# Gate batches of a language-model tower overlap, and the top-k constants of its mixer load and are set at other places

## The reference, cut to what matters

```python
# layer 0, first half (x is the layer norm of the embedded tokens h)
u = silu(x @ u_w.T + u_b); v = silu(x @ v_w.T + v_b)
out = irfft(rfft(v) * rfft(kernel))                    # [b, n, 192]
out = u * out @ o_w.T + o_b                            # gate: elementwise product, then projection
x_r = silu(srms((x - out) @ t_w.T + t_b, 192))         # root-mean-square norm over 64 channels
h = h + (x + x_r)
# layer 0, second half (x is the layer norm of h), per head and token
q = x @ Wq_pk; sim = q . pk_keys                       # two halves of 64 keys
scores, idx = top_k(sim, 16); best 16 of the pairs; softmax; gather keys and values
h = h + causal_attention(...) @ Wo
# layer 1: attention and 8 experts, top 2
```

## Time and profile before

| | us |
|---|---|
| median of 3 runs | 3780.31 (3778.2 to 3783.99) |
| the profiled execution | 3773.41 |
| its span, first to last instruction | 3771.6 |
| mean granted TensorE clock | 0.888 of full speed |
| PE busy | 3106.3 (82%) |
| DVE busy | 2982.6 (79%) |
| ACT busy | 2002.6 (53%) |
| POOL busy | 2063.7 (55%) |
| gate stage | 325 to 447 |
| mixer stage | 447 to the end |

### The profile page before, as it was taken

How to read it: one execution, slowest core, us unless ns; L and a number is a source line. 1 busy time by engine, 2 the same in 40 slices (tenths; PEclk the granted TensorE clock), 3 DMA queues, 4 the chain that set the end, 5 groups by cost and what they waited for, 6 DMA issues and landing times.

```text
span 3771.6 us, 42602 instructions
## 1 busy us (share of the span) xinstructions
PE 3106.3 (82%) x10352; PEld 1432.1 (38%) x10352; DVE 2982.6 (79%) x11187; ACT 2002.6 (53%) x4529; POOL 2063.7 (55%) x2084
## 2 busy tenths in 40 slices
PE   3796326689888897989898979898988889899888
PEld 1453102234334343434343434343443343444334
DVE  4443499899999999899898999898979999965322
ACT  2212215566666666656667666566665666566122
POOL 3000017777777777767565777675646776766000
PEclk9997558799899998999998989899988999999666
DMA  0120101222222221212121222121212221211000
GB/s 15 34 67 18 48 12 51 74 56 67 60 61 67 56 69 51 69 44 71 40 69 36 63 57 65 47 65 47 62 38 57 64 63 50 64 51 45 3 0 3
DMA packets 87060, 186.55 MB, mean 49 GB/s; under 512 B 40216, under 2 KB 42173, under 8 KB 86816
## 3 DMA queue, kind: packets, MB, share of 16 engines
q0 software_dynamic: 66560, 135.40, 13.7%
q1 hardware_dynamic: 20256, 48.48, 4.1%
HBM read 182.69 MB, written 1.05 MB: 49 GB/s over the span
## 4 chain that ended last, share of the span: by engine, by line
DVE 44%; PE 33%; issue 5%; ACT 3%; POOL 2%; DMA 1%; SPq 0%; DVEq 0%; ACTq 0%; POOLq 0%
DVE mx_W L1382 9%; PE mx_acc L1052 8%; PE mx_O L1064 6%; DVE mx_G L1539 5%; PE mx_area L1098 4%; DVE mx_mx_part L1562 3%; POOL mx_G L1021 2%; DVE mx_S L1399 2%; PE mx_D L1042 2%; DVE mx_I L1398 2%; DVE mx_hot L1509 1%; PE mx_area L1114 1%; DVE mx_row L1511 1%; DVE mx_V L1394 1%; PE mx_area L1128 1%
## 5 line engine op out<-in xcount | busy, mean ns | idle before, releaser
L1021 POOL DMA_INDIRECT mx_G<-in_kv_table,mx_slot_i x2048 | 2032.7, 993 | 1396.3 <-issue 553.5
L1052 PE MATMUL mx_acc<-mx_W,mx_table 128*128 128x512 f32 x2048 | 1129.0, 634 | 0.0
L1299 ACT ACTIVATE mx_G<-mx_G,mx_slot_w 128x128 f32<-128x128 f32 x2048 | 702.8, 395 | 313.8 <-DMA mx_G<-in_kv_table,mx_slot_i 313.8
L1382 DVE SCALAR_TENSOR_TENSOR mx_W<-mx_D,mx_W 128x512 f32<-128x512 f32 x1024 | 704.1, 688 | 159.8 <-ACT mx_W L1233 126.5
L1233 ACT ACTIVATE mx_W<-mx_D 128x512 f32<-128x512 f32 x1024 | 605.7, 592 | 350.0 <-PE mx_D L1042 344.1
L1042 PE MATMUL mx_D<-mx_U,mx_pick_b 96*128 96x512 bf16 x1024 | 415.5, 406 | 191.1 <-DVE mx_W L1382 190.5
L1052 PEld LDWEIGHTS mx_acc<-mx_W,mx_table 128*128 128x128 f32 x2048 | 418.6, 206 | 199.3 <-issue 103.5
L1257 ACT ACTIVATE mx_PT<-mx_area 128x512 f32<-128x512 f32 x480 | 243.7, 508 | 324.8 <-PE mx_area L1102 176.2
L1064 PE MATMUL mx_O<-mx_PT,mx_KVs 128*65 128x512 f32 (+3 forms) x768 | 313.9, 490 | 9.2 <-ACT mx_PT L1257 7.4
L1539 DVE TENSOR_TENSOR mx_G<-mx_G 128x1024 f32<-128x1024 f32 (+2 forms) x384 | 299.6, 780 | 17.5 <-ACT mx_G L1299 5.6
L1078 PE MATMUL mx_area<-mx_KTa,mx_QTa 64*128 64x512 f32 (+3 forms) x384 | 202.7, 612 | 124.0 <-DVE mx_mx_part L1562 81.7
(11 more groups left out here) (343 smaller groups left out, 4667.5 us busy)
## 6 DMA issues: line engine op xcount, KB each, us to landing
mx_table<-in_kv_dense SPq DMA_DIRECT2D x64, 512.0 KB, 3.6
mx_G<-in_kv_table,mx_slot_i POOLq DMA_INDIRECT x2048
cv_table<-in_c_idft SPq DMA_DIRECT2D x12, 512.0 KB, 3.3
cv_table<-in_c_dft SPq DMA_DIRECT2D x6, 512.0 KB, 3.4
cv_table<-in_c_idft SPq DMA_DIRECT2D x4, 256.0 KB, 3.2
out_h<-mx_xc SPq DMA_DIRECT2D x4, 256.0 KB
mx_G<-in_c_pick SPq DMA_DIRECT2D x1, 672.0 KB
st_h<-in_tok_W,em_ids POOLq DMA_INDIRECT x32, 2.4
```

Of the source, the lines that this page charges most:

```text
L1021: pool.indirect_dma_start(G[g % RING][:, r, :], None, a["kv_table"], bass.IndirectOffsetOnAxis(slot_i[n % 2][:, k, r:r + 1], 0))\
L1052: pe.matmul(acc[:, :], table[:, tile, :], W[c % TILE_RING][:, :], start=(tile == 0), stop=(tile == TILES - 1)).then_inc(applied, 1)
L1299: last = act.activation(rows, rows, ACT.Copy, scale=slot_w[n % 2][:, k, i:i + 1])
L1382: dve.scalar_tensor_tensor(W[c % TILE_RING][:, :], D_ps[c % 3][:, :], 0.0, W[c % TILE_RING][:, :], ALU.is_ge, ALU.mult).then_inc(w_done, 1)
```

## The change

The gate stage loses its hardware loops and is written out for the 4 batches, with other orders on each engine. PE does `gated(b + 1)`, which is steps 2 and 4 of the next batch, between step 6 of this batch and step 8 of this batch. ACT does step 3 of the next batch right behind the Silu of this one. DVE does step 5 of the next batch and step 1 of the batch after that behind its layer norm. The transposes of `xn` go to `uyT2_ps` and no longer to `outT_ps`. A copy of `xn` back to the tile of the same name in the outer scope (L696) is gone. SP issues the loads of `pk_w` and `keys` in the gate stage, into tiles that live as long as the program. In the mixer PE, ACT and DVE no longer wait at the start: they do so at position 18, where DVE also sets the constants.

```diff
@@ gate_stage, SP
+            sp.dma_start(st["pk_w"][:, :, :], a["pk_w"].rearrange("p (c k) -> p c k", c=HP)).then_inc(keys_in, 16)
+            sp.dma_start(st["keys"][:, :, :], a["pk_keys"].rearrange("p (c k) -> p c k", c=HP)).then_inc(keys_in, 16)
+            sp.wait_ge(keys_in, 32)
@@ gate_stage, PE
-            with pe.Fori(0, B) as b:
+            def gated(b):
                 pe.wait_ge(uy_ready, b + 1)
+                if b >= 2:
+                    pe.wait_ge(xnT_copied, b - 1)
                 for t in range(NB):
                     pe.transpose(uyT1_ps[:, t * P:(t + 1) * P], uy[:, t, 0:P], ident[:, :])
                     last = pe.transpose(uyT2_ps[:, t * P:(t + 1) * P], uy[:, t, P:D1], ident[:, :])
                 last.then_inc(uyT_ready, 1)
                 pe.wait_ge(uyT_copied, b + 1)
-                pe.wait_ge(xnT_copied, b + 1)
...
+            gated(0)
+            for b in range(B):
                 pe.wait_ge(dT_ready, b + 1)
...
                 last.then_inc(z_ready, 1)
+                if b + 1 < B:
+                    gated(b + 1)
                 pe.wait_ge(xn_ready, b + 1)
-                flip_rows(pe, outT_ps, xn, ident).then_inc(xnT_ready, 1)
+                flip_rows(pe, uyT2_ps, xn, ident).then_inc(xnT_ready, 1)
@@ gate_stage, ACT
+            def copy_gated(b):
+                act.wait_ge(uyT_ready, b + 1)
+                if b:
+                    act.wait_ge(outT_ready, b)
...
+            copy_gated(0)
+            for b in range(B):
                 act.wait_ge(square_ready, b + 1)
...
                 act.activation(xr[:, :, :], zn[:, :, :], ACT.Silu).then_inc(xr_ready, 1)
+                if b + 1 < B:
+                    copy_gated(b + 1)
                 act.wait_ge(ln_var, b + 1)
@@ gate_stage, DVE
+            gate_rows(0)
+            differ(0)
+            gate_rows(1)
+            for b in range(B):
...
-                chain.link(dve.tensor_copy(st["xn"][:, blocks, :], xn[:, :, :]))
...
+                if b + 1 < B:
+                    differ(b + 1)
+                if b + 2 < B:
+                    gate_rows(b + 2)
@@ mixer_stage, SP
-        N_LOADS = 16
+        N_LOADS = 14
+        CONSTS = 18
...
-                (pk_w[:, :, :], a["pk_w"].rearrange("p (c k) -> p c k", c=HP)),
-                (keys[:, :, :], a["pk_keys"].rearrange("p (c k) -> p c k", c=HP)),
@@ mixer_stage, PE
-            pe.wait_ge(loaded, 16 * N_LOADS)
-            pe.wait_ge(consts_set, 1)
...
             for q in range(SLOTS * SLOT):
                 c = q - SLOT
+                if q == CONSTS:
+                    pe.wait_ge(loaded, 16 * N_LOADS)
+                    pe.wait_ge(consts_set, 1)
@@ mixer_stage, ACT
-            act.wait_ge(consts_set, 1)
             for q in range(SLOTS * SLOT):
                 t, p = divmod(q, SLOT)
+                if q == CONSTS:
+                    act.wait_ge(consts_set, 1)
@@ mixer_stage, DVE: the wait, the casts and memsets are now constants()
                 if p == 0:
                     chain.clear()
+                if q == CONSTS:
+                    constants()
```

More of the change, by code:

```diff
@@ L656, in _ @@
                 act.activation(xr[:, :, :], zn[:, :, :], ACT.Silu).then_inc(xr_ready, 1)
+                if b + 1 < B:
+                    copy_gated(b + 1)
                 act.wait_ge(ln_var, b + 1)
                 act.activation(stat[:, 3, :], stat[:, 0, :], ACT.Sqrt).then_inc(ln_std, 1)
-                act.wait_ge(xnT_ready, b + 2)
-                act.activation(st["xnT"][:, bass.ds(b * N, N)], outT_ps[:, :], ACT.Copy).then_inc(xnT_copied, 1)
-                chain.clear()
+                act.wait_ge(xnT_ready, b + 1)
+                act.activation(st["xnT"][:, b * N:(b + 1) * N], uyT2_ps[:, :], ACT.Copy).then_inc(xnT_copied, 1)
         @block.vector
@@ L665, in _, with gate_rows, differ @@
             chain = Chain(dve, dve_steps)
+            def gate_rows(b):
+                if b:
+                    dve.wait_ge(uyT_ready, b)
+                dve.tensor_tensor(uy[:, :, :], st["u"][:, b * NB:(b + 1) * NB, :], st["y"][:, :, b * D1:(b + 1) * D1],
+                                  ALU.mult).then_inc(uy_ready, 1)
+            def differ(b):
+                dve.wait_ge(outT_ready, b + 1)
+                if b:
+                    dve.wait_ge(z_ready, b)
+                dve.tensor_tensor(dT[0:D, :], st["xnT"][:, b * N:(b + 1) * N], outT_ps[:, :], ALU.subtract)\
+                   .then_inc(dT_ready, 1)
             dve.memset(uyT2[D:D + 1, :], 1.0).then_inc(ones_set, 1)
             dve.memset(dT[D:D + 1, :], 1.0).then_inc(ones_set, 1)
[L668 to L671, removed]
-                   .then_inc(uy_ready, 1)
-                dve.wait_ge(outT_ready, b + 1)
-                dve.tensor_tensor(dT[0:D, :], st["xnT"][:, bass.ds(b * N, N)], outT_ps[:, :], ALU.subtract)\
-                   .then_inc(dT_ready, 1)
+            gate_rows(0)
+            differ(0)
+            gate_rows(1)
+            for b in range(B):
+                blocks = slice(b * NB, (b + 1) * NB)
                 dve.wait_ge(z_ready, b + 1)
@@ L687, in _ @@
                 chain.link(dve.tensor_tensor(xc[:, :, :], h1[:, :, :], xr[:, :, :], ALU.add))
-                chain.link(dve.tensor_copy(st["h"][:, blocks, :], xc[:, :, :]))
+                chain.mark(dve.tensor_copy(st["h"][:, blocks, :], xc[:, :, :]))
                 layernorm_a(dve, chain, xc[:, :, :], h1[:, :, :], sq[:, :, :], stat)
@@ L809, in mixer_stage @@
         pick_b = m.sb("pick_b", [96, 14, P], BF16)
-        pk_w = m.sb("pk_w", [D, HP, P])
-        keys = m.sb("keys", [P, HP, 4 * NK])
+        pk_w, keys = st["pk_w"], st["keys"]
         rank = m.sb("rank", [P, CAND])
@@ L1671, in tower @@
             "xnT": m.sb("xnT", [D, T]),
+            "pk_w": m.sb("pk_w", [D, HP, P]),
+            "keys": m.sb("keys", [P, HP, 4 * NK]),
         }
```

48 lines of the change are left out of this document (23 added, 25 removed).

## The result

The changed kernel takes 3728.92 us in the median of 4 runs (3714.7 to 3733.95), the kernel before, run beside it, 3782.15 (3778.2 to 3785.09, 4 runs). The ratio is 0.9854, with a 95% interval from 0.9823 to 0.9884. The forecast was 3728.6. The difference of the medians is 53.2 us, by the interval 44 to 67.

A forecast was written before the change was run, and what follows sets the result against it. The prediction took the gate stage and the mixer's head as chains on the path, the rest as full. Savings of 38.8 + 12.9 = 51.7 us from 3780.3 gave 3728.6 us, range 3718 to 3743.

The forecast's parts named there:

- the forecast's own case: Gate stage saves 38.8 us and mixer's head 12.9, giving 3728.6 us; chance 0.61.
- The period: Gate stage: time between `z` copies of successive batches, summed to 16.6 us from 29.5, saving 38.8 us over three.
- The mis-sized term: Gate stage: PE's flips of `xn` take 1.7 us per period and hide DVE's 1.21 us for `dT`.
- the point on TensorE's queue: Gate stage: matmuls stay in program order, so `z` can't pass the flips; passing would save 1.5 us in all.
- The sign that the prediction gave beside it: Gate stage: PE goes from projection to flips to `z` without a stop, at a granted clock near 1.
- rival 2: Gate stage: clock stays high, DVE sets a 14.4 us period, 58.3 us saved in all, time 3722.0; chance 0.12.
- The mixer's head: From SP's first mixer issue to k = 15: 35.4 us instead of 48.3, saving 12.9 us.
- the loops: Gate stage: replacing three hardware loops counted at nothing, with up to 0.8 us per DVE turn off the path.
- carried over: Whole kernel: the median lies 6.9 us above the profiled execution before, and the forecast assumed the same after.
- Rival 3: Mixer's head: late loads or the constants leave none of the 12.9 us, time 3741.5; chance 0.06.
- rival 4: Mixer: waits for gathers or table parts lose half the lead, time 3754; chance 0.03.
- rival 5: Mixer: TensorE's clock is granted less and loses 59.3 us or more, so the kernel is slower; chance 0.01.

The follow-up runs named there:

- z_first: The changed kernel with PE doing `z` of the next batch ahead of the flips of this batch: 3725.77 us, ratio 0.9867.
- warm_fill: The changed kernel plus unread matmuls on PE between transposes and projection of batches 1 to 3: 3724.38 us, ratio 0.9843.
- consts_first: The changed kernel with the wait and constants back at position 0, `pk_w` and `keys` still loaded early: 4225.17 us, ratio 0.9893, in the slow session.
- memsets_early: The changed kernel with the constants' memsets moved to positions 0 and 4, only the four casts left at position 18: 3724.03 us, ratio 0.9849.
- written_out: The kernel before with its three gate-stage hardware loops written out, old order, nothing overlapped: 3775.34 us, run once.
- after_same: The changed kernel again, unedited, timed beside `both_again`: 3724.84 us, ratio 0.9856.
- gate_only: The new gate stage with the old mixer head, against the kernel before: 4236.63 us, ratio 0.9912, in the slow session.
- head_only: The old looped gate stage with early loads and the constants at position 18, against the kernel before: 4252.02 us, ratio 0.996, in the slow session.
- both_extra: The changed kernel with the edits of both `warm_fill` and `memsets_early`: 3720.25 us, ratio 0.9834.
- both_again: The kernel of `both_extra` run again, beside `after_same`: 3719.64 us, ratio 0.9837.
- late_start: The kernel of `both_extra` with 14 more scratch memsets on DVE ahead of the gate stage: 3723.34 us, ratio 0.9852.
- the first four experiments: `gate_only`, `head_only`, `consts_first` and `after_again`, measured in one session in which every kernel took 4190 to 4290 us, the one before 4271.75.
- after_again: The changed kernel without an edit, run in the slow session: 4215.9 us, ratio 0.9876.

## Why the prediction was right

The forecast of 3728.6 us was right, within 0.4 us of the median, and the forecast's own case was the one that happened. That it agrees to 0.4 us is luck, as the last point shows; what the prediction can claim is the mechanism and the 51.7 us, for 53.2 measured. By its steps:

- **The period.** From the start of the first `z` copy to that of the second the trace has 4.53 us to the end of the Silu, 1.91 to the projection, 6.89 to DVE's `dT`, 1.21 of `dT` and 2.09 of `z`: 16.63. The forecast had 4.5 + 2.0 + 6.3 + 1.7 + 2.1 = 16.6. The other two periods are 15.13 and 16.12, since the projection takes 5.4 and 6.4 us in them. The stage saved 40.8 us in this execution and 38.8 was forecast; over the profiled executions of the changed kernel it was 47.9 to 49.5 us long, which is 39.1 to 40.8 saved.
- **The mis-sized term** is "1.7" for the flips, with "DVE's 1.21 us for `dT` run beside the flips and are hidden by them". It is the other way round. With the high clock the flips took 1.26 us (356.13 to 357.39) and ended before `dT` (357.54); `z` waited 0.20 us for `dT`. The term on the path is `dT`'s 1.21 us, 0.5 less per period, which is 1.5 of the 1.9 us by which the three periods beat the forecast. The 1.7 came from a spacing of 0.13 us between transposes, read at the rows where the clock was just changing (390.68 to 390.81); at the high level they are 0.11 us apart (359.55 and 359.66 in the trace after), and the flips go from 2.3 to 1.26 us, not to 1.7. From this follows that the point on TensorE's queue was without effect: `z`'s input came last, so no run here shows whether a matmul could pass another, and `z_first` shows PE waiting for `dT` with the flips out of the way.
- **The clock.** The forecast put the projection in the middle between both levels, at 6.3 us, which held for the mean of three (6.9, 5.4 and 6.4): 0.53 to 0.66 in it, 1.00 behind it. The sign that the prediction gave beside it, a clock near 1 from the projection on, contradicts its own 6.3 and didn't come. The "pause of some 3 us per period" was 3.3 us once and 4.7 twice. `warm_fill` shows that this pause is what brings the clock down: with matmuls in it the projection is at 1.00 and the mechanism of rival 2 takes over, with a period of 13.6 where 14.4 was worked out. Of the 0.8 us between them 0.5 is again the 1.7, since `z` started 1.2 us behind `xn`, and 0.2 is the way up to `xn`, 10.4 us for 10.6. The Trainium skill, "TensorE: Matmul & The Clock Gate", part 1, which calls throttled the default state that activity releases, agrees with this run.
- **The mixer's head** saved 12.9 us as forecast (48.34 to 35.40), and every run with this head took 35.39 to 35.41. The constants were an unbroken block of 8.5 us on DVE, 26.8 us behind SP's first issue, with no wait for a transfer. `consts_first` shows the place of the constants, which hides the wait for the other loads, as the larger part, and `memsets_early` that 7.1 of the 8.5 us could go as well.
- **Costed at nothing**: the loops. The forecast allowed "up to 0.8 us of gain per turn of DVE's loop (...), off the path now". `written_out` shows 1.6 us per turn in the old order, 0.6 of it that idle time. This isn't an error of the sum, because the new period was rebuilt from durations that held no loop, but it bears on what the 38.8 us are owed to: if the loops would cost the same in the new order, which no run shows, some 4.9 us of the stage's 39.1 to 40.8 come from them and some 35 from the order. The copy at L696, put at nothing, was never tried alone.
- **The rest**. The mixer from k = 15 to the end was to keep its length, 3276 us. In the profiled execution it took 3272.6, in `after_same` 3280.5. The step "carried over" added 6.9 us from the profiled execution to the median; after the change the median lies 14.2 above the profiled execution, 7.3 more. The profiled execution itself (3714.7) was 7.0 under the forecast for it, 3721.7. These two misses cancel in the forecast of the median. Of the 7.0, 2.0 are the stage, 3.7 the mixer, 1.0 that its first `z` copy came earlier (343.00 for 344.00) and 0.3 the way from the last one to SP's issue.

Of the other signs, the wait at `uyT2_ps` did not come (ACT's copy to `xnT` ends at 358.46, the next transposes start at 359.43), k = 0 came 5.5 us behind SP's issue for 5.7, and two of the three periods were within the 16 to 17 us.

Rival 3 (nothing of the head), rival 4 (half of the lead lost) and rival 5 (slower) did not occur; `gate_only` and `head_only` together show both parts in the result.

## What to carry to other kernels

A stage in which no engine is busy half of the time is a chain: write down one period from the rows, each piece with the wait that ends it, and let the next batch's work start in the waits; the sum then gave the time to 1.5 us per batch here. In such a stage TensorE's clock is a term of its own, since a pause of 3.3 to 4.7 us ahead of a matmul group here doubled the time of its first matmuls, and of two chains of nearly equal length (here flips and `dT`) the sum must take the later one at the clock that will be granted, not the one that the old trace shows. A spacing of instructions is read where the clock is steady. Constants are best written where their engine waits for something else, and a load that the first instruction of a stage needs belongs into the stage before, so that the wait for the rest can move behind work that doesn't need it.

## What the runs showed beyond that

The length of the mixer, whose instructions are the same, varies from execution to execution and hides small gains at the end. From k = 15 to the end the profiled executions took 3276.3 (before), 3272.6 (after), 3284.1 (`memsets_early`), 3286.8 (`warm_fill`), 3297.1 (`both_extra`), 3278.3 (`written_out`), 3280.5 (`after_same`), 3287.3 (`both_again`), 3276.7 (`z_first`) and 3276.4 us (`late_start`). Part of it is the clock where PE is densest. Two windows of PE in the trace of the kernel before, 20 us of the same kind of work in two parts of the program (the granted clock stands behind the count of matmuls):

```profile
1994.00:2014.00 20.00, 19.24 (x92) 0.98 0.11 30
2763.30:2783.30 20.00, 19.73 (x66) 0.58 0.08 20
```

and PE's timeline of that kernel there, the pause ahead of each and the same pairs of instructions at either level:

```profile
1991.89 2.08 PE L1142 MATMUL mx_X<-mx_keys,mx_qpk 128*128 128x256 f32 x4 [3.74 <-ACT mx_S L1269]
...
2000.61 1.12 PE L1126 MATMUL mx_area<-mx_q_w,mx_KTa 1*128 1x512 f32 x2
2001.66 1.16 PE L1128 MATMUL mx_area<-mx_w,mx_PT 128*128 128x128 f32 x8
...
2761.08 2.07 PE L1142 MATMUL mx_X<-mx_keys,mx_qpk 128*128 128x256 f32 x4 [2.79 <-ACT mx_S L1269]
...
2773.69 2.07 PE L1126 MATMUL mx_area<-mx_q_w,mx_KTa 1*128 1x512 f32 x2
2775.69 2.08 PE L1128 MATMUL mx_area<-mx_w,mx_PT 128*128 128x128 f32 x8
```

PE is busy in both windows to over 95% and is granted the low level in most of one of them. In both places PE had paused twice just before, for 2.2 and 3.7 us in the first and 2.1 and 2.8 in the second. In the first the high level was back after some 3 us of work, in the second only near 2780, 19 us after the last pause. This makes the way from one query projection (L1138) to the next 120.1 us long instead of 113.1. I didn't expect the low level to last through a part where PE hardly pauses.

The two ways, measured so in each profiled execution, are 113.1 and 120.1 (before), 118.1 and 113.0 (after), 120.2 and 112.3 (`memsets_early`), 120.2 and 113.2 (`warm_fill`), 117.7 and 120.2 (`both_extra`), 121.0 and 121.0 (`written_out`), 120.1 and 113.1 (`after_same`), 119.9 and 113.1 (`both_again`), 113.0 and 112.6 (`z_first`), 113.3 and 113.2 us (`late_start`). So each can be either, in kernels with the same code there. The two explain part of the mixer's spread and not all: `late_start`'s mixer was 20.7 us shorter than that of `both_extra`, of which they are 11.4, but `written_out` has both long and a mixer of only 3278.3 us. What decides the level stays open: chance in each execution, or where such a stretch falls after the start. The first way began at 1926.3 us in `after_same`, where it was long, and at 1927.5 in `late_start` and 1928.0 in `z_first`, where it was short. The time up to the gate stage varies as well: the first `z` copy of all kernels but `late_start` starts anywhere from 342.6 to 349.3 us. Why 16 us of lead at k = 15 are only 5 us in the medians is therefore argued by this spread, not shown.

In the session of the first four experiments, the mixer took longer in every profiled kernel (3757 to 3781 us from k = 15), and the times of the kernel before say the same of it. The durations of the instructions of DVE and ACT are unchanged. Single engines pause up to 10 us at waits whose releaser the profile doesn't find on the core ("remote"), and there are moments in which PE, DVE, ACT and POOL all do nothing: eight of 0.5 to 2.1 us between 1000 and 1400 us of `after_again`, none in the trace after. The waits of `after_again`:

```profile
DVE mx_W L1411 <- remote: 155.9, 49, 5.0
POOL mx_G L1048 <- DVE mx_W L1411: 810.3, 363, 32.4
```

The second row is 350.8 us in the trace after. A later session under the same chip number had the usual 3779.86 us for the kernel before, so it doesn't go with the chip number; I didn't find the cause, and it is why a kernel must be compared with the one before in its own session.
